# Attention scores from scaled 16-bit pairs, with the keys' and values' pairs made in halves on ScalarE and GpSimd

## What is computed

```python
xn = _layernorm(x)
x = x + _L0_attn_ref(xn, Wq, Wkr, Wdk, Wupk, Wupv, Wo) + _L0_ffn_ref(xn, W_gate, W_up, W_down)
# attention: 2 batches, 1024 positions, 32 query heads and 8 key/value heads of 128
q = (xn @ Wq.T)                       # turned by the rotary tables
k = parts of (xn @ Wkr.T), turned, and of (xn @ Wdk.T) @ Wupk.T
v = ((xn @ Wdk.T) @ Wupv.T)
scores = where(causal, q k^T / sqrt(128), -1e9)      # 4 query heads share a key/value head
out = (softmax(scores) v) @ Wo.T
# feed-forward: 512 -> 1792 -> 512
out = (silu(xn @ Wg.T) * (xn @ Wu.T)) @ Wd.T
```

## Time and profile before

| | us |
|---|---|
| median of 3 runs | 2282.2 (2280.94 to 2282.47) |
| the profiled execution, its own time | 2282.42 |
| its span, first to last instruction | 2280.6 |
| TensorE busy | 2238.7 (98%) |
| VectorE busy | 1574.2 (69%) |
| ScalarE busy | 1108.8 (49%) |
| GpSimd busy | 974.3 (43%) |

### The profile page before, as it was taken

The page is one execution under the profiler, slowest core; times in us unless marked ns, Lnnn a source line. Parts: engine busy times, 40 slices in busy tenths (PEclk is TensorE's granted clock), DMA queues, the critical chain, the costliest instruction groups (busy, mean ns, idle before and its releaser), DMA issues.

```text
span 2280.6 us, 33617 instructions
## 1 busy us (share of the span) xinstructions
PE 2238.7 (98%) x11776; PEld 1461.6 (64%) x11776; DVE 1574.2 (69%) x3680; ACT 1108.8 (49%) x2184; POOL 974.3 (43%) x808
## 2 busy tenths in 40 slices
PE   8999999998999999999999999999999999999998
PEld 6566675754666666666666666666666666666655
DVE  6666555546777777777777777777777777777765
ACT  3423425244555555555555555555455555555544
POOL 4001020203545455545454554555454545454542
PEclk9999999999999999999999999999999999999999
DMA  5857677596110202020211132220202020202000
GB/s 209 310 155 268 187 224 269 182 337 224 28 61 24 65 23 67 19 69 16 70 37 53 51 98 64 72 61 24 65 20 68 22 65 20 70 23 67 15 27 20
DMA packets 88198, 213.59 MB, mean 94 GB/s; under 512 B 9312, under 2 KB 25952, under 8 KB 81376
## 3 DMA queue, kind: packets, MB, share of 16 engines
q1 hardware_dynamic: 85920, 207.27, 28.5%
q10 hardware_dynamic: 2112, 4.19, 0.5%
HBM read 156.89 MB, written 54.53 MB: 93 GB/s over the span
## 4 chain that ended last, share of the span: by engine, by line
PE 90%; DVE 4%; issue 3%; ACT 2%; POOL 1%; DMA 0%; SPq 0%; DVEq 0%; ACTq 0%; POOLq 0%
PE ob L1341 16%; PE scores L1315 16%; PE qb L1295 13%; PE ob L1352 13%; PE ptb L1327 11%; PE ring L1068 8%; PE ring L1048 6%; PE down L1077 4%; PE ring L1103 2%; ACT short_prob L1184 1%; DVE acc L1266 1%; DVE q_sin L1243 1%; ACT oT L1201 1%; DVE q_cos L1245 1%; DVE q_sin L1244 0%
## 5 line engine op out<-in xcount | busy, mean ns | idle before, releaser
L1198 ACT ACTIVATE pT<-ptb 128x512 f16<-128x512 f32 x576 | 333.9, 591 | 422.7 <-PE ptb L1327 422.4
L1249 DVE SCALAR_TENSOR_TENSOR pT<-ptb,pT 128x512 f16<-128x512 f32 x576 | 390.6, 688 | 81.4 <-ACT pT L1198 76.6
L1341 PE MATMUL ob<-pT,v 128*128 128x512 f16 x1728 | 439.4, 380 | 0.1
L1315 PE MATMUL scores<-kT,late_qT 128*128 128x384 f32 (+3 forms) x1536 | 365.9, 373 | 9.7 <-DVE nmax L1228 8.7
L1163 POOL TENSOR_TENSOR long_prob<-long_prob,rinv 128x384 f32<-128x384 f32 (+3 forms) x256 | 304.2, 1201 | 156.3 <-DVE rinv L1273 155.9
L1169 POOL TENSOR_TENSOR q_cos<-q_cos,q_sin 128x512 f32<-128x512 f32 x124 | 157.5, 1270 | 480.1 <-DVE q_cos L1245 480.1
L1352 PE MATMUL ob<-wo,oT 128*128 128x512 f16 x1536 | 353.6, 380 | 3.5 <-DVE oT L1253 3.5
L1163 POOL TENSOR_TENSOR short_prob<-short_prob,rinv 128x512 f32<-128x512 f32 (+3 forms) x256 | 277.6, 1095 | 180.5 <-DVE rinv L1273 178.5
L1295 PE MATMUL qb<-xT,wq 128*128 128x512 f16 x1488 | 349.3, 379 | 0.0
L1315 PEld LDWEIGHTS scores<-kT,late_qT 128*128 128x128 f32 x1536 | 265.0, 189 | 44.9 <-POOL late_qT L1173 13.4
L1184 ACT ACTIVATE long_prob<-long_prob,nmax 128x384 f32<-128x384 f32 (+3 forms) x256 | 204.7, 800 | 167.6 <-DVE nmax L1228 165.2
(11 more groups left out here) (117 smaller groups left out, 2732.6 us busy)
## 6 DMA issues: line engine op xcount, KB each, us to landing
wq<-w_halves SPq DMA_DIRECT2D x126, 256.0 KB, 3.1
ff_raw<-in_ffw SPq DMA_DIRECT2D x56, 384.0 KB, 5.4
k_parts<-stage SPq DMA_DIRECT2D x128, 128.0 KB, 2.5
w_fetch<-in_wqo SPq DMA_DIRECT2D x16, 1024.0 KB, 5.6
w_fetch<-in_wqo SPq DMA_DIRECT2D x32, 512.0 KB, 4.6
w_halves<-w_parts SPq DMA_DIRECT2D x32, 512.0 KB, 3.1
kT<-k_parts SPq DMA_DIRECT2D x32, 512.0 KB, 5.7
wo<-w_halves SPq DMA_DIRECT2D x16, 1024.0 KB, 4.9
```

Of the source, the lines that this page charges most:

```text
L1198: nc.scalar.activation(pT[:, t % 4, HI], ptb[t % 2][:], ACT.Copy, scale=P_SCALE).then_inc(pT_hi, 1)
L1249: nc.vector.scalar_tensor_tensor(pT[:, t % 4, LO], ptb[t % 2][:], P_SCALE, pT[:, t % 4, HI], ALU.mult, ALU.subtract).then_inc(pT_split, 1)
L1315: mm = nc.tensor.matmul(sc[:, c * 512:c * 512 + cols], q[:, x, i % AHEAD * P:i % AHEAD * P + P], kT[e % 2][:, y, c * cols:(c + 1) * cols], ...
L1341: mm = nc.tensor.matmul(ob[:], v16[e % 2][:, x, j], pT[:, t % 4, y], start=(j == 0 and (x, y) == (HI, HI)), stop=(is_last(kind, n, j) and ...
```

## The change

Scores take pairs of 16-bit floats for queries and keys, in place of float32r pairs, and:

- Keys are stored unsplit (`k_rows`), and VectorE takes their largest absolute value where it made their low part before. One scale for all keys is found in the last chunk (`top_of_keys`, `weight_scales(KEY)`, with two small transfers). Its inverse, the queries' scale and the sign go into `score_scale`, a column of SBUF that takes the place of the constant -1.0 in the masking instruction. The scaling of the query tables on GpSimd goes; the tables carry a constant factor.
- The pair of a head's keys is made in stage two in two halves of 512 positions. ScalarE scales a half in place, then copies it to 16 bits (KH, two instructions each), and GpSimd subtracts (KL). Values are done likewise (VH with two instructions, VL now on GpSimd). The planner gets KH and KL from the last scores of units 3 and 4, VH and VL from those of units 5 and 6, with the rank of VH and VL before. For the first head all of it stands in the feed-forward blocks 7, 8, 10 and 11 of the last chunk.
- The load of keys is half as large, and one buffer takes it.

```diff
+K_UNITS, V_UNITS = (3, 4), (5, 6)
-def values_split(kind, n, j):
-    if kind == "Q" and n == 2:
-        return [("act", "VH", 0, 0, 1.1, 0.1), ("dve", "VL", 0, 0, 1.15, 0.1)]
-    if kind == "S" and n % TB == TB // 2 and j == 0 and n // TB + 1 < B * KVH:
-        return [("act", "VH", n // TB + 1, 0, 1.1, 0.1), ("dve", "VL", n // TB + 1, 0, 1.15, 0.1)]
+def pieces_split(kind, n, j):
+    ge, pos = n // TB + 1, n % TB
+    if kind == "S" and j == GRP - 1 and ge < B * KVH:
+        for units, hi, lo in ((K_UNITS, "KH", "KL"), (V_UNITS, "VH", "VL")):
+            if pos in units:
+                half = units.index(pos)
+                return [("act", hi, ge, half, 1.3, 0.1), ("pool", lo, ge, half, 1.27, 0.05)]
...
-        late_qT = sb("late_qT", 67 * KB, [P, GRP, 2, 512], F32R)
+        late_qT = sb("late_qT", 67 * KB, [P, GRP, 2, 512], F16)
...
-        kT = [sb(f"kT{e}", (115 + 72 * e) * KB, [P, 2, S], F32R) for e in range(2)]
+        kT = [sb(f"kT{e}", (115 + 4 * e) * KB, [P, 2, S], F16) for e in range(2)]
+        k32 = sb("k32", 99 * KB, [P, S])
...
+        def key_hi(act, ge, h):
+            act.wait_ge(k_loaded, 16 * ge + 16)
...
+            nc.scalar.activation(k32[:, half], k32[:, half], ACT.Copy, scale=w_scale[:, KEY:KEY + 1])\
+                .then_inc(k_scaled, 1)
+            act.wait_ge(k_scaled, 2 * ge + h + 1)
+            nc.scalar.activation(kT[ge % 2][:, HI, half], k32[:, half], ACT.Copy).then_inc(k_hi, 1)
+        def key_lo(pool, ge, h):
+            pool.wait_ge(k_hi, 2 * ge + h + 1)
...
+            nc.gpsimd.tensor_tensor(kT[ge % 2][:, LO, half], k32[:, half], kT[ge % 2][:, HI, half], ALU.subtract)\
+                .then_inc(k_split, 1)
...
+                    if c == CHUNKS - 1:
+                        if m in (7, 8):
+                            key_hi(act, 0, m - 7)
+                        if m in (10, 11):
+                            value_hi(act, 0, m - 10)
...
-                    if c == CHUNKS - 1 and m == 11:
-                        value_scales()
+                        if m == 10:
+                            value_scales()
...
-                        mask[:, S - W:].rearrange("p (a c) -> p a c", a=parts), -1.0, 3e38, ALU.add, ALU.min,
+                        mask[:, S - W:].rearrange("p (a c) -> p a c", a=parts), score_scale[:, 0:1], 3e38, ALU.add, ALU.min,
```

More of the change, by code:

```diff
@@ L178, in is_last @@
     return kind == "PV" and j == key_blocks(n) - 1
-URGENT = {"T": 0, "PV": 0, "W": 0, "NORM": 0, "INV": 1, "QL": 1, "EXP": 2, "S": 2, "Q": 3, "VH": 4, "VL": 4}
+URGENT = {"T": 0, "PV": 0, "W": 0, "NORM": 0, "INV": 1, "QL": 1, "EXP": 2, "S": 2, "Q": 3, "KH": 4, "KL": 4, "VH": 4, "VL": 4}
 def rank(kind, n):
@@ L222, in product_needs @@
         head = n * GRP + j - 2
-        return [("pool", "QL", query_of(n, j), 0)] + ([("dve", "S", head // GRP, head % GRP)] if head >= 0 else [])
+        return [("pool", "QL", query_of(n, j), 0)] + ([("dve", "S", head // GRP, head % GRP)] if head >= 0 else []) + \
+            ([("pool", "KL", n // TB, 1)] if j == 0 and n % TB == 0 and n else [])
     if kind == "T":
@@ L280, in orders @@
             note(pe_free, "pe", None)
-            for chain in (followers(*event), values_split(*event)):
+            for chain in (followers(*event), pieces_split(*event)):
                 if chain:
@@ L447, in program @@
         acc_ready = [sem(f"acc_ready{i}") for i in range(TB)]
-        k_loaded = [sem(f"k_loaded{e}") for e in range(2)]
+        k_loaded = sem("k_loaded")
+        k_scaled = sem("k_scaled")
+        k_hi = sem("k_hi")
+        k_split = sem("k_split")
         v_loaded = sem("v_loaded")
@@ L646, in chunk @@
                     if n == G_KN and c in (1, 2):
[L647 to L649 removed]
+                        load_top(c - 1)
+                    if last and n == G_V + 3:
+                        store_top(KEY)
+                    if last and n == G_V + 7:
+                        load_top(KEY)
                     if n == G_V + 5:
@@ L666, in chunk @@
                                 head, row = 2 * (n - G_KN) + q // 2, q % 2 * HALF + RH
-                            sp.dma_start(scr["k"][head, row:row + RH, c], stage[q * RH:(q + 1) * RH, s].bitcast(F32))\
+                            sp.dma_start(scr["k"][head, row:row + RH, c], stage32[q * RH:(q + 1) * RH, s, HI])\
                                 .then_inc(stored[s], 16)
@@ L746, in keys_gpsimd @@
                     rstd_of(c + 1)
-            wait(pool, tab2, 16)
-            wait(pool, w_scale_ready, 4)
-            nc.gpsimd.tensor_scalar(qtab[:], qtab[:], q_unscale[:, 0:1], None, ALU.mult).then_inc(qtab_scaled, 1)
+            for h in range(2):
+                key_lo(pool, 0, h)
+            for h in range(2):
+                value_lo(pool, 0, h)
         def keys_scalar(act):
@@ L784, in keep_hi @@
                     wait(act, stored[s], (c + 1) * (16 * stores_upto(s, GROUPS)))
-                wait(act, w_scale_ready, 4 if kind == QUERY else 7)
+                wait(act, w_scale_ready, 3 * kind + 3)
                 nc.scalar.activation(w_parts[:, p, 0, :, HI], w_fetch[:, k % 2, 0:2], ACT.Copy,
```

161 lines of the change are left out of this document (99 added, 62 removed).

## The result

| | before | after |
|---|---|---|
| median, us | 2282.1 | 2329.2 (2328.3 to 2330.1, 4 runs) |
| ratio to before | | 1.0207 (1.0189 to 1.0225) |
| span of the profiled execution | 2280.6 | 2327.4 |
| mean granted clock | 0.999 | 0.983 |
| waits of unit 4's first T, first 15 heads | none | 15 of some 3.75 us |

The changed kernel is 2.1% slower; the forecast was 2325 us. In the text, "before" and "after" also name the two kernels. "Head" stands for key/value head from here on.

The account below looks back on a forecast made before the run. TensorE, busy 98% of the span, was taken as the bound. 2282.4 + 56.3 (wait) + 17 (clock) - 27 (scores) - 2 - 1.6 (rest) = 2325.1, so 2325 us; range 2298 to 2348, likeliest case 2305 to 2343.

Parts of the forecast that it names:

- wait at unit 4's first T: Unit 4's first T waits for the fourth NORM, now behind Q's addition: 3.75 us, 15 times, +56.3 us.
- clock behind it: TensorE at half clock behind the new waits: 1.7 us lost in two of three, +17 us, bounds 0 and 27.
- 16-bit scores: TensorE's score matmuls get cheaper: 2.2 us a head, 1.8 left outside waits, 15 times, -27 us.
- unit 4's last scores: Their 0.82 us wait stays: VL goes, the query's low part still holds them; 0, bounds 0.8 gained, 0.5 lost.
- opening, last chunk, last head: First head's first units and last head -2; VL leaving the opening -2; smaller key stores -1; last chunk +1.4 us.
- The same loss behind most of them: Clock loss behind the new waits at unit 4's first T, taken as 1.7 us in two of three.
- the two cases of before: TensorE waits of 2.50 and 2.63 us in the old trace, with 3.4 and 3.6 us at half speed.
- Rival 1: The wait at unit 4's first T comes, the clock stays: 2308 us, chance 0.20.
- the line over 384 columns: Score matmul price extrapolated from 512 and 448 columns, 0.44 ns a column: 0.188 us at 448, 0.048 at 128.
- Rival 3: 16-bit score matmuls are no faster than 32-bit ones and all 15 slow stretches come: 2364 us, chance 0.08.
- Costed at nothing: New KH, KL, VH, VL work and score_scale's up to 57 ns per masking instruction: hidden by spare engine time, 0.
- Rival 2: The wait at unit 4's first T does not come and the kernel gets faster: 2234 us, chance 0.09.

Follow-up runs that it names:

- experiment 3: After with 17 needless matmuls (3.67 us) on TensorE in front of unit 4's first T, filling the wait: 2296.7 us, ratio 1.0069 to before.
- experiment 1: After with unit 4's last INV on VectorE and last NORM on GpSimd moved ahead of Q in the first 15 heads: 2253.8 us, ratio 0.9878 to before.
- experiment 6: Before with the 15 mid-stream VL on VectorE placed behind the Q item instead of ahead of it: 2276.8 us, ratio 0.9977 to before.
- experiment 2: After with only VectorE's last INV of unit 4 moved ahead of Q, NORM left behind Q's addition: 2329.3 us, ratio 1.0209 to before.
- experiment 5: After with only GpSimd's fourth NORM of unit 4 moved ahead of Q's addition, INV left behind Q: 2300.7 us, ratio 1.0085 to before.
- experiment 4: Before with only the order changed: Q ahead of unit 4's last INV on VectorE and last NORM on GpSimd: 2363.5 us, ratio 1.0360 to before.
- experiment 9: After with unit 4's last INV and NORM ahead of Q, and constant -1.0 replacing the score_scale column in masking: 2253.5 us, ratio 0.9876 to before.
- experiment 7: After with TensorE's W of unit 3 moved ahead of unit 4's first T in 15 heads, lists unchanged: 2263.3 us, ratio 0.9922 to before.
- experiment 8: After with unit 4's last INV and NORM ahead of Q, and KL moved behind that NORM on GpSimd: 2254.5 us, ratio 0.9880 to before.
- experiment 10: After with unit 4's last INV and NORM ahead of Q, and W of unit 3 ahead of unit 4's first T: 2253.9 us, ratio 0.9875 to before.

## Why the prediction was right, and which term was mis-sized

Forecast 2325 us, measured 2329.2. The spans differ by 46.8 us; the prediction's sum was 42.7. Term by term:

| term | predicted (bounds), us | measured, us | from |
|---|---|---|---|
| wait at unit 4's first T | +56.3 (54 to 60) | +55.2 | 15 x 3.68: from Q to T 7.49 us, in before 3.81 |
| clock behind it | +17 (0 to 27) | +31.1 | T to second T above 3.08 us; experiment 3: 32.5 |
| T to second T at full clock | not in the sum | +0.8 | 15 x 0.06: 3.08 us in experiments 1 and 3, 3.02 in before |
| 16-bit scores | -27 (-12 to -45) | -31.4 | 15 x 2.09: experiment 1, see below |
| unit 4's last scores | 0, inside the bounds above | -5.4 | 15 x 0.36 (0.82 to 0.46), experiment 6 |
| opening, last chunk, last head | -3.6 | -3.2 | the first head's Q ahead of unit 4's T starts at 600.13, was 603.31 |

The measured terms sum to +47.1, 0.3 us more than the spans give. The 2.09 of the scores is what the period of experiment 1, which has no half-speed stretch, leaves: it is 1.61 us shorter than before's, although 0.78 is lost on the way from Q to T (4.59 us for 3.81) and 0.06 to the second T, and 0.36 of it is the gain at unit 4's last scores.

That the sum came within 5 us is in part luck. The clock was put 14 us too low, and the gains of the scores and of unit 4's last scores, put some 10 us too low together, hid most of that. The stated span of 2305 to 2343 us doesn't follow from the bounds of the terms either: with all of them at the low or at the high end the sums are 2283 and 2359.

**The wait** came as worked out: at its place, 15 times, T 3.68 us later where 3.75 was taken, with the path Q on TensorE, Q on VectorE, addition, NORM. Experiments 2 and 5 show that both lists are in the path, and 5 that the wait is 1.15 us shorter, about GpSimd's addition (1.27), when only NORM is moved. What the prediction read from the printed order was what ran. A detail was misread: the prediction has a matmul drain for 0.3 us, and in after it is 0.17 (1265.30 + 1.30 - 1266.43), so 3.60 us were listed as idle and not 3.5.

**The clock** is the term that was mis-sized, by 14 us and beyond its own bound of 27. "The same loss behind most of them" was too little in two ways. The share: a half-speed stretch stands behind 30 of 30 waits of 3.7 us (after, experiment 4), and behind 13 of 15 of 2.6 us, so two thirds was a guess below both. The length: the two cases of before had both some 3.4 us, and the prediction took that for the size of a stretch. In after it is some 6.8 us behind six of the waits (2.8 to 2.95 us lost in each; the rest of it lies inside the wait, as the prediction said it might) and some 3.4 behind nine (1.4 to 1.7 lost; where all of the stretch lies behind T, 2 x 1.69 = 3.4). What makes one or the other is open: in experiment 4, with waits 0.08 shorter, all 15 are of the short kind. The length of the wait alone doesn't decide either whether a stretch comes. In the last head 2.76 us of idle are listed before T in after and in experiment 1 alike; in after it then takes 1.12 us, at half speed,

```profile
2262.93 1.12 PE L1404 MATMUL ptb<-ident,short_prob 128*128 128x128 f32 x4 [2.76 <-POOL short_prob L1245]
```

and in experiment 1 it takes 0.66, at full speed:

```profile
2188.48 0.66 PE L1414 MATMUL ptb<-ident,short_prob 128*128 128x128 f32 x4 [2.76 <-POOL short_prob L1255]
```

Rival 1, the wait without the clock, is out: the half-speed rows are in the trace, and experiment 3 gets their time back.

**The scores** gained more than predicted. For 448 columns the price is 0.189 us (1276.49 to 1277.62 in after's timeline, 1.13 for six), as the line predicted with 0.188. For 128 columns it is 0.056, not the 0.071 that was taken: the saving is some 0.045, not 0.03, close to the bound that the line over 384 columns gave. With 0.014 to 0.016 for 384 to 512 and 0.010 for 256 and 320 the saving of a head comes to some 2.3 us, of which 0.08, the first scores of unit 5, lie in the shadow of the wait. The period gives 2.09, and the 0.1 to 0.2 between them stay open. The Trainium skill (TensorE: Matmul & The Clock Gate, "Back-to-back issue gap") has two figures for this; the form of columns over 2.4 GHz plus 2.5 ns gives 0.056 at 128 and 0.189 at 448. The trace agrees with it at both, and not with the 81 ns. Rival 3 is out.

**Unit 4's last scores.** The prediction saw both holders, VL and the query's low part, and took their sum as unchanged. VL's went (0.82 to 0.46). The expected delay of 0.3 to 0.4 by KH did not show: its two instructions run from 1252.55 to 1253.92, and ScalarE then still stands idle for 3.70 us before unit 4's exponential, behind which it makes the query's high part:

```profile
1252.55 0.71 ACT L518 ACTIVATE k<-k,w_scale 128x512 f32<-128x512 f32 x1
...
1258.51 0.83 ACT L1270 ACTIVATE short_prob<-short_prob,nmax 128x640 f32<-128x640 f32 x1 [3.70 <-DVE nmax L1310]
```

GpSimd's low part itself became shorter, 1.16 us for 1.28, in the groups by shape of after, for the earlier trace rows:

```profile
L1255 POOL TENSOR_TENSOR late_qT<-q_cos,late_qT 128x512 f16<-128x512 f32 x63 | 72.9, 1157 | 57.7 <-ACT late_qT L1275 57.7
```

**Costed at nothing.** `score_scale` costs 60 ns an instruction, as predicted, and 0.1 us in a head where nothing hides it (experiment 9). KL on GpSimd holds up NORM by 0.2 us in experiment 1, and nothing in after, where the longer path covers it. The saving of the last stretch is hidden: from unit 4's first T in the fifteenth head to the end both kernels take 173.1 us, but in after 2.8 of them are lost in the half-speed stretch behind that T, which the table counts under the clock. Rival 2, a kernel that is faster since the wait does not come, is out, and experiment 1 made such a kernel: the rival gave 2234 us, measured were 2253.8. The 0.85 us left at T and the 0.47 left at unit 4's last scores, which rival 2 had at nothing, are 15 x 1.32 = 20 us.

## What to carry to other kernels

- Where engines run fixed lists, print the lists around each step on which the bottleneck waits, and look for an item that has moved behind something that the bottleneck itself must first produce. Here the serial path from there, summed from the old trace, was right to a tenth of a microsecond. It cost 55 us, 86 with the clock, where the arithmetic gained 31.
- Price an idle stretch of TensorE as its length plus a loss of clock: here 1.4 to 3.0 us behind 43 of 45 waits of 2.6 us or more (first 15 heads of after and of experiments 4 and 5), nothing behind the 15 of 1.2 us in experiment 7 and the 15 of 0.85 in experiment 1. Moving work that TensorE has anyway into the gap (experiment 7) takes back both.
- When different repairs of one wait give the same period to the hundredth (here experiments 1, 8 and 10), the next limit is already there; follow the first wait behind the repaired one.

## What the hardware showed that was not expected

- The half-speed stretches behind the 15 waits of after are of two kinds, some 6.8 us (six) and some 3.4 us (nine), though the waits are alike to 0.01 us; the windows of 18 us show a clock of 0.81 and of 0.91.
- A score matmul of 128 columns costs 0.056 us on 16-bit pairs and 0.101 on float32r pairs, 45% less; at 448 columns it is 0.189 and 0.202.
- GpSimd's subtraction that writes 128 x 512 results in 16 bits takes 1.16 us, with float32r 1.28 us.
